# Output projection, last norm and routed FFN in one stage, and K and V laid out in DRAM for contiguous loads

## The reference, cut to what matters

```python
h = _layernorm(x) * (1 + ca) + sa
q, k, v = (h @ W.T + b).reshape(B, S, 32, 16)      # for Wq, Wk, Wv
scores = einsum('bshd,bsgd->bshg', q, k) / 4        # 32 x 32 heads of each token
attn = softmax(where(scores > 0.001, scores, -inf))
x = x + ga * (einsum('bshg,bsgd->bshd', attn, v).reshape(B, S, 512) @ Wo.T + bo)
h = _layernorm(x) * (1 + cb) + sb
logits = h @ route_w.T                              # 8 experts, the best one is used
x = x + gb * (one_hot(argmax) * top * (h @ A)) @ Bw # rank 16 for each expert
```

## Time and profile before

| | us |
|---|---|
| runs: median (lowest to highest) | 2551.21 (2549.51 to 2552.23) |
| the profiled execution: its own time | 2552.01 |
| its span | 2550.4 |
| PE busy | 2029.6 (80%) |
| DVE busy | 1572.9 (62%) |
| POOL busy | 1108.5 (43%) |
| ACT busy | 1029.2 (40%) |

### The profile page before, as it was taken

One profiled execution on the slowest core, in us unless ns is written; L12 is line 12 of the kernel. 1 busy time (PEld: TensorE's weight loads), 2 busy tenths in 40 slices (PEclk: granted clock), 3 DMA queues, 4 the chain that ended last, 5 costly groups with the idle time before them and its releaser, 6 DMA issues. The chain is left out here.

```text
span 2550.4 us, 34479 instructions
## 1 busy us (share of the span) xinstructions
PE 2029.6 (80%) x11904; PEld 1680.7 (66%) x11904; DVE 1572.9 (62%) x3747; ACT 1029.2 (40%) x2380; POOL 1108.5 (43%) x866
## 2 busy tenths in 40 slices
PE   7489999999999942954447999999999996357634
PEld 1378888888888832743335888888888885346434
DVE  1666666666666669244645666666666666852645
ACT  1255555555555522122114555555555553131211
POOL 0454555555554534132325555555554544341322
PEclk9699999999999976965768999999999999678566
DMA  5300100010001001285031100010001001024921
GB/s 228 108 17 26 42 18 26 18 41 26 17 26 42 17 30 54 79 91 125 15 119 34 33 17 26 21 39 25 17 26 42 17 26 38 23 72 90 94 87 42
DMA packets 188903, 123.30 MB, mean 48 GB/s; under 512 B 107172, under 2 KB 151204, under 8 KB 187700
## 3 DMA queue, kind: packets, MB, share of 16 engines
q1 hardware_dynamic: 174356, 101.26, 16.1%
q10 hardware_dynamic: 14368, 19.78, 2.4%
HBM read 100.01 MB, written 21.01 MB: 47 GB/s over the span
## 5 line engine op out<-in xcount | busy, mean ns | idle before, releaser
L965 POOL TENSOR_TENSOR gqa_rot<-gqa_rot,consts 128x512 f32<-128x512 f32 x160 | 209.1, 1307 | 640.8 <-ACT gqa_rot L786 640.7
L802 ACT ACTIVATE gqa_prob<-gqa_prob,gqa_nmax 128x128 f32<-128x128 f32 (+3 forms) x512 | 282.0, 552 | 198.6 <-DVE gqa_nmax L887 198.6
L887 DVE CUSTOM_DVE_ANT_0 gqa_prob<-gqa_pS,consts 128x128 f32<-128x128 f32 (+3 forms) x512 | 220.2, 486 | 73.6 <-PE gqa_pS L686 72.6
L430 PE MATMUL ln_pT<-consts,ln_xn 128*128 128x128 f32 x256 | 59.8, 422 | 253.9 <-DVE ln_xn L409 253.9
L895 DVE TENSOR_TENSOR gqa_ptl<-gqa_pT,gqa_pth 128x384 fp32r<-128x384 f32 (+1 forms) x384 | 218.3, 597 | 31.7 <-ACT gqa_pth L812 27.1
L430 PEld LDWEIGHTS ln_pT<-consts,ln_xn 128*128 128x128 f32 x256 | 51.3, 225 | 262.3 <-DVE ln_xn L409 262.3
L812 ACT CAST gqa_pth<-gqa_pT 128x384 fp32r<-128x384 f32 (+1 forms) x384 | 182.7, 511 | 94.4 <-PE gqa_pT L701 94.3
L968 POOL TENSOR_TENSOR gqa_full<-gqa_full,gqa_rot 128x512 f32<-128x512 f32 x160 | 206.7, 1292 | 12.6
L740 PE MATMUL gqa_pW<-woh,gqa_oh 128*128 128x512 f32 x504 | 202.7, 402 | 9.0 <-DVE first_y L912 9.0
L659 PE MATMUL gqa_pj<-first_hh,wqh 128*128 128x512 f32 x496 | 205.5, 414 | 0.0
L740 PE MATMUL gqa_pW<-woh,gqa_ol 128*128 128x512 f32 x504 | 197.3, 392 | 0.0
(11 more groups left out here) (221 smaller groups left out, 5299.9 us busy)
## 6 DMA issues: line engine op xcount, KB each, us to landing
raw_q<-in_wq SPq DMA_DIRECT2D x16, 1024.0 KB, 5.3
raw_o<-in_wo SPq DMA_DIRECT2D x16, 1024.0 KB, 5.1
mod_wm<-in_wmod SPq DMA_DIRECT2D x8, 1536.0 KB, 19.9
raw_kv<-in_wkv SPq DMA_DIRECT2D x16, 512.0 KB, 6.5
x<-in_x SPq DMA_DIRECT2D x4, 1024.0 KB, 6.4
kp<-qkv_rest SPq DMA_DIRECT2D x16, 256.0 KB, 2.3
qp<-qkv_rest SPq DMA_DIRECT2D x16, 256.0 KB, 2.3
vp<-qkv_rest SPq DMA_DIRECT2D x16, 256.0 KB, 2.3
```

The costliest lines, as they stand in the source:

```text
L802: ins = nc.scalar.activation(p, p, ACT.Exp, scale=-1.0, bias=nmax[r][:, i:i + 1], accum_out=den[r][:, i:i + 1])
L887: nc.vector.tensor_tensor_reduce(prob[r][:, P_OFF[i]:P_OFF[i] + w], pS[s][:, c:c + w], held.mask[:, T - w:T], -1.0, LARGEST, ALU.add, ALU.min,
L965: nc.gpsimd.tensor_tensor(rot[r % 2][:], rot[r % 2][:], held.sinT, ALU.mult).then_inc(sined, 1)
```

## The change

Three edits.

1. `OutWeights` is new, and its load and split, and those of `LoraWeights`, move into the head attention (`ahead`): SP issues their four DMAs after the V loads of the third unit, ACT and POOL split them behind their last chunk.
2. The three stages behind the head attention become one, `stage_finish`, without barriers between its parts and with two sequences offset against each other. The bias times the gate is added to x by POOL ahead of time, DVE evicts the projection by a multiplication with the gate and adds it to x. Three PSUM banks serve the projection and both FFN products in the order of `users`. The statistics, Newton steps, choice of expert and eviction are the same operations as before, for each sequence apart.
3. V is stored in DRAM as `[sequence, 4, 32 heads, 32, 4, 17]`, with the ones, so that each head's values of a unit are contiguous. `heads_kd` and `heads_bd` get another order of dimensions in SBUF. A K load is then 16 runs of 4,096 bytes and a V load 32 runs of 2,176 bytes. A V item is stored with four DMAs of 32 x 32 runs of 68 bytes instead of one. `QKV_ORDER` becomes V, K, Q.

The memsets of ones go from POOL and DVE in the head attention; four on DVE come in `stage_qkv`. The 24 items, all matmuls of the three products and the chunks of the head attention stay the same in number and size.

The Q/K/V projection, the weights and their order:

```diff
-QKV_ORDER = (1, 0, 2)
+QKV_ORDER = (2, 1, 0)
...
+    def load(self, sp):
+        sp.dma_start(self.raw[:], self.a["w1o"].rearrange("(k p) n -> p k n", p=P)).then_inc(self.came, 16)
...
+    def his(self, act):
+        act.wait_ge(self.came, 16)
+        for k in range(KT):
+            self.nc.scalar.copy(self.wh[:, k], self.raw[:, k]).then_inc(self.hi, 1)
...
+        for k in range(KT):
+            pool.wait_ge(self.hi, k + 1)
+            self.nc.gpsimd.tensor_tensor(self.wl[:, k], self.raw[:, k], self.wh[:, k].bitcast(F32), ALU.subtract).then_inc(self.lo, 1)
...
                     sp.wait_ge(turned, n + 1)
-                    src = rest[n % NB]
                     if w == 2:
-                        dst = a["vp"][b].rearrange("(t r) x -> r t x", r=KT)[m]
-                        sp.dma_start(dst, src[:]).then_inc(stored[n % NB], 16)
+                        for r in range(4):
+                            sp.dma_start(a["vp"][b, r, :, :, m].rearrange("g l x -> l g x"),
+                                         values(n)[r * LO:(r + 1) * LO]).then_inc(stored[n % NB], 16)
                     else:
                         dst = a["kp" if w == 1 else "qp"][b, :, 4 * m:4 * m + 4].rearrange("j d l x -> (d l) j x")
-                        sp.dma_start(dst, src[:].rearrange("p (j x) -> p j x", j=4)).then_inc(stored[n % NB], 16)
+                        sp.dma_start(dst, rest[n % NB][:, 0:T].rearrange("p (j x) -> p j x", j=4)).then_inc(stored[n % NB], 16)
...
-                        if n - 8 < FIRST_V:
-                            pe.wait_ge(left, n - 7)
+                        if n - 8 < NV:
+                            pe.wait_ge(turned, n - 7)
                         else:
-                            pe.wait_ge(turned, n - 7)
+                            pe.wait_ge(left, n - 7 - NV)
...
-                for n, (w, b, m) in enumerate(items[:FIRST_V]):
+                for n in range(NV, N):
+                    w, b, m = items[n]
...
-                    if n >= NB:
+                    if n >= NV + NB:
                         act.wait_ge(turned, n - NB + 1)
...
+                for i in range(NB):
+                    nc.vector.memset(values(i)[:, :, D1:], 1.0).then_inc(ones, 1)
...
-                        dve.wait_ge(stored[n % NB], 16 * (n // NB))
-                    if n < FIRST_V:
-                        dve.wait_ge(left, n + 1)
-                        nc.vector.transpose(rest[n % NB][:], flat[n % NB][:]).then_inc(turned, 1)
+                        dve.wait_ge(stored[n % NB], stored_by[n - NB])
+                    if n < NV:
+                        dve.wait_ge(full, n + 1)
+                        nc.vector.tensor_tensor(values(n)[:, :, 0:D1], ps[n % 8][:].rearrange("p (g x) -> p g x", g=H1),
+                                                vbias[:].rearrange("p (g x) -> p g x", g=H1), ALU.add).then_inc(turned, 1)
                     else:
-                        dve.wait_ge(full, n + 1)
-                        nc.vector.tensor_tensor(rest[n % NB][:], ps[n % 8][:], vbias[:], ALU.add).then_inc(turned, 1)
+                        dve.wait_ge(left, n - NV + 1)
+                        nc.vector.transpose(rest[n % NB][:, 0:T], flat[n % NB][:]).then_inc(turned, 1)
```

The head attention:

```diff
+        kd = [st.sb(f"kd{i}", [P, 4, 4 * LU, H1]) for i in range(NU)]
+        bd = [st.sb(f"bd{i}", [P, 4, 4 * LU, VW]) for i in range(NU)]
...
-                eng.dma_start(kd[u % NU][D1 * j:D1 * j + D1, :, j], a["kp"][b, j, :, ls, :].rearrange("d l (r h) -> d (l r) h", h=H1)
+                eng.dma_start(kd[u % NU][D1 * j:D1 * j + D1, j], a["kp"][b, j, :, ls, :].rearrange("d l (r h) -> d (l r) h", h=H1)
...
+                eng.wait_ge(v_zeroed[u], 1)
             for r in range(4):
-                t0 = (LO * r + l0) * KT
-                src = a["vp"][b, t0:t0 + KT * LU, :].rearrange("t (g x) -> g t x", g=H1)
-                eng.dma_start(bd[u % NU][32 * r:32 * r + 32, :, r, 0:D1], src).then_inc(v_in[u], 16)
+                src = a["vp"][b, r, :, l0:l0 + LU].rearrange("g l j x -> g (l j) x")
+                eng.dma_start(bd[u % NU][32 * r:32 * r + 32, r], src).then_inc(v_in[u], 16)
 
...
+                        for weights in ahead:
+                            weights.load(sp)
...
-                                           kd[u % NU][0:ROWS, 4 * (l0 + l) + r].rearrange("p j g -> p (j g)"), start=True, stop=True)
+                                           kd[u % NU][0:ROWS, :, 4 * (l0 + l) + r, :], start=True, stop=True)
                     mm.then_inc(s_full, 1)
...
+                            mm = pe.matmul(pO[c % NO][32 * j:32 * j + 32, l], pt[c % NR][:, 4 * l + j, :],
+                                           bd[u % NU][:, :, s0 + 4 * l + j, :], start=True, stop=True)
                     mm.then_inc(o_full, 1)
 
...
+                for weights in ahead:
+                    weights.his(act)
```

The new last stage (the bodies that do the same as before are left out):

```diff
-def stage_attention_out(nc, held, a, half):
-
-    with Stage(nc, "wo1") as st:
...
+def stage_finish(nc, held, a, out, ws, half):
...
+        users = ([("o", j) for j in range(NT)] + [("a", j) for j in range(TT)] + [("b", j) for j in range(TT)]
+                 + [("a", j) for j in range(TT, NT)] + [("b", j) for j in range(TT, NT)])
...
+                pool.wait_ge(bo_in, 16)
+                pool.wait_ge(ga_in, 16 * HB)
+                for b in range(HB):
+                    nc.gpsimd.tensor_tensor(bg[:, b], bo[:], ga[:, b], ALU.mult).then_inc(bias_gated, 1)
                 for j in range(NT):
-                    pool.wait_ge(gated, j + 1)
-                    nc.gpsimd.tensor_tensor(x[:, j, :], x[:, j, :], yg[j % 2][:], ALU.add).then_inc(added, 1)
+                    pool.wait_ge(bias_gated, j // TT + 1)
+                    nc.gpsimd.tensor_tensor(x[:, j, :], x[:, j, :], bg[:, j // TT], ALU.add).then_inc(biased, 1)
...
+                def project(b):
+                    pe.wait_ge(at_lo, (b + 1) * KT)
...
+                def turn(b):
+                    if b:
+                        pe.wait_ge(scaled, b * KT)
+                    for j in range(b * TT, (b + 1) * TT):
+                        pe.wait_ge(xn_done, j + 1)
+                        for k in range(KT):
...
+                def turn_weights(b):
+                    pe.wait_ge(routed, b + 1)
+                    if b:
+                        pe.wait_ge(w_lo, b)
...
+                project(0)
+                project(1)
+                turn(0)
+                down(0)
+                turn(1)
+                turn_weights(0)
+                up(0)
+                down(1)
+                turn_weights(1)
+                up(1)
...
+                def features(b):
+                    t = slice(b * T, (b + 1) * T)
...
+                    act.wait_ge(o_full, (b + 1) * TT)
+                    for k in range(KT):
+                        nc.scalar.activation(hf[:, k, t], pT[k][:], ACT.Identity, bias=held.modh[:, 1, 2, k, b:b + 1],
+                                             scale=held.modh[:, 1, 3, k, b:b + 1]).then_inc(scaled, 1)
+                        act.wait_ge(scaled, b * KT + k + 1)
+                        nc.scalar.copy(hh[:, k, t], hf[:, k, t]).then_inc(h_hi, 1)
...
+                features(0)
+                lowered(0)
+                features(1)
+                weight_his(0)
+                lowered(1)
+                weight_his(1)
...
+                def residual(b):
+                    for j in range(b * TT, (b + 1) * TT):
+                        dve.wait_ge(o_full, j + 1)
+                        nc.vector.tensor_tensor(yg[j % 3][:], bank("o", j)[:], ga[:, b], ALU.mult).then_inc(o_gated, 1)
+                        dve.wait_ge(o_gated, j + 1)
+                        dve.wait_ge(biased, j + 1)
+                        nc.vector.tensor_tensor(x[:, j, :], x[:, j, :], yg[j % 3][:], ALU.add).then_inc(x_new, 1)
+                        dve.wait_ge(x_new, j + 1)
+                        nc.vector.bn_stats(stats[:, j, :], x[:, j, :]).then_inc(stat_done, 1)
...
+                    residual(b)
+                    normalise(b)
+                for b in range(HB):
+                    choose(b)
+                    finish(b)
```

More of the change, by code:

```diff
@@ L1051 @@
 LO = 32
+VW = D1 + 1
 def stage_qkv(nc, held, a, ws):
@@ L1062, in stage_qkv @@
         flat = [st.sb(f"flat{i}", [P, T]) for i in range(NB)]
-        rest = [st.sb(f"rest{i}", [P, T]) for i in range(NB)]
+        rest = [st.sb(f"rest{i}", [P, H1 * VW]) for i in range(NB)]
         ps = [st.ps(f"ps{i}", [P, T]) for i in range(8)]
-        w_lo, b_scaled, full, left, turned = (st.sem(n) for n in ("w_lo", "b_scaled", "full", "left", "turned"))
+        w_lo, b_scaled, ones, full, left, turned = (st.sem(n) for n in ("w_lo", "b_scaled", "ones", "full", "left", "turned"))
         stored = [st.sem(f"stored{i}") for i in range(NB)]
@@ L1309, in _ @@
                 nc.vector.memset(bd[0][:], 0.0).then_inc(v_zeroed[0], 1)
-                dve.wait_ge(v_zeroed[0], 1)
-                for r in range(4):
```

(43 more changed lines are left out.)

290 lines of the change are left out of this document (151 added, 139 removed).

## The result

The changed kernel took 2517.54 us (median of 4 executions, 2517.28 to 2518.79) where the kernel before took 2551.72: a ratio of 0.9868, 95% interval 0.9854 to 0.9882. It is 34 us faster. The forecast was 92 us, and 2517.5 lies just outside its range.

The account below looks back on a forecast made before the run. Loads were taken to pace the head attention, and barrier-closed handover chains the last three stages. Per pass 18.2 (loads) + 28.7 (merge) - 0.8 (V stores), twice, is 92.2 us off 2552.0, forecast 2459 us; range 2438 to 2515.

Parts of the forecast that it names:

- The last stage: Output projection, last norm and FFN merged: 88.5 us instead of 117.2, 28.7 us won a pass, bounds 22 to 33.
- the 1.5 us for handovers: Merged last stage: allowance for handovers not listed, added to 87 us to give 88.5.
- The loads: Head attention: contiguous K and V loads put DVE last, 18.2 us won a pass, bounds 12 to 22.
- four weight loads add 2.0: Head attention: the weights' four loads add 2.0 us of issue on SP before the later K loads.
- the lower bound: Head attention: only 12 us won a pass, if landings stay near 5 and the weights' 1.3 MB delay unit 4.
- My list of DVE's first maxima: Head attention: start of DVE's first maximum of each unit, 11.2 to 31.1 us from the loads, then 37.0, 42.8, 48.7.
- The V stores: Projection stage: 32,768 short writes a pass at 23 ns a packet, 5.9 us an item, cost 0.8 us a pass.
- 25 + 8s: Projection stage: its length in us when V stores set the pace, s being the price of one V item.
- just hidden: Projection stage: at s = 5.9 the stores give 72 us, inside the stage's 73.1 + 0.8; they surface at 6.1.
- 30 ns (2483): Rival, projection stage: V stores as dear as 512-byte writes, 24 us more in total, 2483 us; chance 0.18.
- 43 ns (2539): Rival, projection stage: each short write pays twice, s = 11.1, 40 us a pass, 2539 us; chance 0.10.
- PE's K waits "under 12": Sign in the head attention: PE's wait for K loads falls from 30.5 to under 12 us.

Follow-up runs that it names:

- layouts_alone: Changed kernel with the three last stages of the kernel before and no weights loaded ahead; new K and V layouts and V first kept: 2543.80 us, ratio 0.9974.
- changed_again: The changed kernel measured once more in a later set, nothing altered: 2496.89 us, ratio 0.9788.
- changed_third: The changed kernel measured a third time in a later set, nothing altered: 2498.93 us, ratio 0.9804.
- one_store_an_item: Changed kernel with each V item stored by one transfer of 128 partitions instead of four of 32, same packets: 2500.2 us, projection 89.2 us.
- two_store_queues: Changed kernel with two of the four stores of each V item issued by ACT instead of SP: 2508.8 us, projection 94.5 us.

## Why the prediction missed

**The last stage: right in sum, by luck in its parts.** 88.5 forecast, 88.5 measured (87.4 to 91.9 over the runs). PE began 6.9 us in, 2.1 earlier than the 9 forecast. ACT's second feature pairs ran from 55.3 to 60.6, forecast 53 to 58, and the cast behind them ended at 61.2, forecast 58.9. So the way from PE's start to that cast was 4.4 us longer than I had added up; the early start, the 1.5 us for handovers and an end 0.8 us shorter made up for it. POOL's additions ended at 25.1 us, forecast 25.

**The loads: the mechanism right, the weights mis-sized.** In "four weight loads add 2.0" I priced the loads by their issue on SP alone and left their bytes, which unit 4's loads queue behind, to the lower bound. My list of DVE's first maxima, with the weights in it, had unit 4 at 31.1 us, chunk 14 at 48.7 and the end at 74.2; layouts_alone, which has no weights there, measured 31.1, 48.7 and 74.2. Without the weights my sum would have DVE itself last from unit 4 on (24.0 + 5.86 = 29.9), 73.0 in all, so part of the exact match is luck, of 1.2 us. With them unit 4 came at 38.1 and chunk 14 at 56.9. The weights cost 8.6 us in this pass (82.8 - 74.2), 5.0 in the first (79.6 - 74.6), 3.5 to 6.0 in the four passes of changed_again and changed_third, and 7.4 on the old layouts. The gain of 9.6 us here is under the 12 of my bound, 15.0 in the first pass is not.

**The V stores: the step that failed.** The formula 25 + 8s held within 1 us for the changed kernel and the other runs with its stores, but for one_store_an_item (2 us under) and two_store_queues (6 under, where ACT was late). The price in it did not: I took 23 ns "nearest to the packets of like size", which were reads, and set the stores' cost at 0.8 us a pass because at 5.9 us an item they were "just hidden". Both rows that I read it from are holds, the one of 512-byte writes at a share of 0.34, where nothing is full, and neither has a write as short. Packed 68-byte writes went at 35 ns (4,096 x 35 / 16 = 9.0 us an item), later at 31, past the 6.1 us an item that the stage hides. That is between my rivals of 30 ns (2483) and 43 ns (2539), each too narrow a point for what is a range. Cost: 24.8 us in this pass and 23.3 in the first, forecast 0.8.

**The sum.** Merged stage 28.7 in this pass and 27.3 in the first, attention 9.6 + 15.0, projection -24.8 - 23.3: 32.5 us, where 33.3 of span were measured and 92.2 forecast. Of the missing 60, 46.5 are the stores, 11.8 the attention (8.6 us short in one pass, 3.2 in the other) and 1.4 the merged stage of the first pass.

My marks in the profile: DVE waiting for stores more than 12 us past the last V item, and an issue of over 1.8 us, both appeared and named the fault. PE's K waits "under 12" was a bad mark: 17 us of them are the start of the stage, and the run with 74.2 us has 19.9 in all, 18.4 of them there.

## What to carry to other kernels

Price a short write to DRAM by a write, and by its exact bytes: start, length, and whether a neighbour shares its line. Here padding 68 bytes to 128 gave back the whole loss of 14 us a pass, for twice the traffic; the tile that reads them has to be as wide, or the loads pay (attention 88.6 against 83.4 us). And a load "ahead" is not free when its queue feeds the stage it hides in: put it where that queue has nothing urgent behind it, and look which wait it meets next.

## What I had not expected of the hardware

64-byte writes went at 12 ns a packet, and crossing a 64-byte line made no difference (12.3 and 12.5). 4 bytes more made it 22, 68 bytes side by side 32 to 39, while 128 bytes took 15. The same instructions on the same data took 97.9 and 97.2 us in the two passes of one set of executions and 88.0 in both of another. 19.1 of the 21.0 us between the two spans lie in the stage of these writes. The runs don't tell whether the chip or the placement does it.
